# First loads, GpSimd's memsets and the first token copy of a gated scan, in another order

## What is computed

```python
def step(h, xt):
    m = jnp.concatenate([xt, h], axis=-1) @ weight + bias
    c = jnp.tanh(m[:, units:])
    g = jax.nn.sigmoid(m[:, :units] + 1.0)
    return g * h + (1.0 - g) * c, ...
x = x + scan(step, cond, x)
x = x + block(x, cond)
```

## Time and profile before

| | us |
|---|---|
| median of 3 runs | 462.07 |
| lowest and highest of them | 461.28, 463.29 |
| span of the profiled execution | 461.8 |
| busy in it: TensorE | 375.0 |
| VectorE | 304.8 |
| ScalarE | 231.7 |
| GpSimd | 78.5 |

### The profile page before, as it was taken

One profiled execution on the slowest core, in us unless ns is written; L12 is line 12 of the kernel. 1 busy time (PEld: TensorE's weight loads), 2 busy tenths in 40 slices (PEclk: granted clock), 3 DMA queues, 4 the chain that ended last, 5 costly groups with the idle time before them and its releaser, 6 DMA issues.

```text
span 461.8 us, 14117 instructions
## 1 busy us (share of the span) xinstructions
PE 375.0 (81%) x5296; PEld 253.9 (55%) x5296; DVE 304.8 (66%) x1938; ACT 231.7 (50%) x1025; POOL 78.5 (17%) x151
## 2 busy tenths in 40 slices
PE   1999899898857896857898999979599899778832
PEld 1755676566746675746666766636344446446510
DVE  5454444576777776777776676653842378699883
ACT  2123422325335425335446455645688878953952
POOL 7000000012000012000012000032210124266580
PEclk9999999999999999999999999985759989995966
DMA  7200840002000000000000000000000000000102
GB/s 179 62 1 4 181 95 3 2 3 48 1 1 3 1 4 1 2 2 1 2 3 3 1 4 1 2 2 2 3 2 3 1 2 4 1 2 1 23 1 68
DMA packets 9114, 8.42 MB, mean 18 GB/s; under 512 B 1276, under 2 KB 7694, under 8 KB 9047
## 3 DMA queue, kind: packets, MB, share of 16 engines
q1 hardware_dynamic: 8950, 7.26, 7.0%
q0 software_dynamic: 96, 0.26, 0.2%
HBM read 6.45 MB, written 1.08 MB: 16 GB/s over the span
## 4 chain that ended last, share of the span: by engine, by line
PE 56%; DVE 22%; ACT 12%; issue 5%; POOL 2%; DMA 1%; SPq 0%; DVEq 0%; ACTq 0%; POOLq 0%
PE zb L804 21%; PE tb L927 6%; PE zb L782 4%; DVE prod_hi L1569 4%; PE tb L751 4%; ACT state L1265 3%; PE firsts L1098 3%; PE firsts L983 2%; ACT prd L1421 2%; PE tb L898 2%; PE zb L1078 2%; PE firsts L967 2%; ACT state L1268 2%; PE zb L788 2%; PE firsts L804 2%
## 5 line engine op out<-in xcount | busy, mean ns | idle before, releaser
L804 PEld LDWEIGHTS zb<-prod_hi,whh 128*128 128x128 f16 x1920 | 73.7, 106 | 89.9 <-DVE prod_hi L1569 85.8
L1265 ACT ACTIVATE state<-zb 128x8 f32<-128x8 f32 x240 | 42.7, 178 | 152.9 <-PE zb L804 152.4
L804 PE MATMUL zb<-prod_hi,whh 128*128 128x8 f16 x1920 | 91.0, 171 | 34.7 <-DVE prod_hi L1569 34.0
L1569 DVE SCALAR_TENSOR_TENSOR prod_hi<-state 128x16 f16<-128x16 f32 x255 | 44.7, 175 | 83.0 <-ACT state L1268 80.1
L804 PE MATMUL zb<-prod_lo,whh 128*128 128x8 f16 x960 | 63.7, 172 | 0.0
L1575 DVE TENSOR_TENSOR prod_lo<-prod,prod_hi 128x16 f16<-128x16 f32 x255 | 44.7, 175 | 8.7
L1421 ACT ACTIVATE prd<-zb 128x640 f32<-128x640 f32 x64 | 42.2, 712 | 7.8 <-PE zb L1078 7.2
L804 PEld LDWEIGHTS zb<-prod_lo,whh 128*128 128x128 f16 x960 | 44.5, 107 | 0.8
L1571 DVE SCALAR_TENSOR_TENSOR prod<-state 128x16 f32<-128x16 f32 x256 | 43.3, 169 | 0.3 <-ACT state L1268 0.3
L1268 ACT ACTIVATE state<-zb 128x16 f32<-128x16 f32 x240 | 42.8, 178 | 0.0
L1577 DVE SCALAR_TENSOR_TENSOR state<-prod 128x8 f32<-128x8 f32 x256 | 40.8, 159 | 0.0
(11 more groups left out here) (378 smaller groups left out, 708.6 us busy)
## 6 DMA issues: line engine op xcount, KB each, us to landing
mod<-ada_rows SPq DMA_DIRECT2D x4, 768.0 KB, 11.8
resid<-in_x_dram SPq DMA_DIRECT2D x6, 128.0 KB, 3.7
ffz<-shift_rows SPq DMA_DIRECT2D x4, 131.0 KB, 3.3
out_dram<-state SPq DMA_DIRECT2D x8, 64.0 KB, 2.1
out_dram<-early SPq DMA_DIRECT2D x8, 64.0 KB, 2.1
yy<-in_L_cond_w_ada_dram SPq DMA_DIRECT2D x1, 384.0 KB
early<-in_L_cond_weight_dram SPq DMA_DIRECT2D x2, 128.0 KB
resid<-in_x_dram POOLq DMA_DIRECT2D x2, 128.0 KB, 3.5
```

What stands on the lines that cost most here:

```text
L804: i = pe.matmul(z_bank(t, k)[:, NB * (t % CH):NB * (t % CH) + NB], whh[:, half, p, k, :], src[:, NB * p:NB * p + NB], start=False, stop=Fa ...
L1265: act.activation(r[:, 24:32], z_bank(t, 1)[:, k:k + NB], ACT.Tanh, scale=-1.0 / ZS)
L1569: dve.scalar_tensor_tensor(prod_hi[:, :], r[:, 16:32], 1.0, r[:, 0:16], ALU.add, ALU.mult).then_inc(hi_ready, 1)
```

## The change

Five things change, all ahead of step 0.

- The SP queue loads w0x second and cond last of the four; cond counts on its own semaphore, and VectorE waits for the other three alone. TensorE waits for cond, not for the weights.
- The two loads of the tokens of chunk 0 are issued by ScalarE, ahead of its other work, and no longer by GpSimd.
- GpSimd waits for `w_split` after the identities and the small constants. It then clears only the upper nine columns of each head's part of V, without waiting for its own end, and goes on to V's column and O as before.
- `first_x_part` runs the bias matmuls for both gates first, then waits for `xT_first` and runs the token matmuls, gate 1 ahead of gate 0.
- The token copy of chunk 0 is two instructions, one for the first 16 steps (128 columns), which sets `xT_first`, and one for the other 48, which sets `xT_sb`. The wait for `xT_sb` moves into `x_part(0)`.

```diff
@@ sync
             sp.dma_start(w0h[:, :], w0[D:2 * D, :]).then_inc(load_scan, 16)
-            sp.dma_start(condr[:, :], cond).then_inc(load_scan, 16)
+            sp.dma_start(w0x[:, :], w0[0:D, :]).then_inc(load_scan, 16)
             sp.dma_start(b0row[:, :], row(b0)).then_inc(load_scan, 16)
-            sp.dma_start(w0x[:, :], w0[0:D, :]).then_inc(load_scan, 16)
+            sp.dma_start(condr[:, :], cond).then_inc(load_cond, 16)
@@ gpsimd
-            for slot in range(2):
-                tile_dma(pool, x, resid, 0, slot, False).then_inc(load_x0, 16)
...
             pool.memset(half_[:, :], 0.5)
-            settled(pool.memset(V[:, :, :, :, :], 0.0))
+            pool.wait_ge(w_split, 1)
+            pool.memset(V[:, :, :, :, VC:VP], 0.0)
             pool.memset(V[:, :, :, :, HD:HD + 1], C_HEAD)
             pool.memset(O[:, :, :, (NC - 1) * P:NC * P], 0.0).then_inc(pool_init, 1)
@@ tensor, first_x_part
                 for k in range(2):
-                    pe.matmul(z_bank(0, k)[:, 0:n], w0s[:, k, :], xT[:, 0:n], start=True, stop=False,
-                              skip_group_check=True)
                     for half in range(2):
                         pe.matmul(z_bank(0, k)[:, 0:n], b0h[:, half, k, :], onesh[:, 0:n],
-                                  start=False, stop=False, skip_group_check=True)
+                                  start=(half == 0), stop=False, skip_group_check=True)
+                pe.wait_ge(xT_first, 1)
+                for k in (1, 0):
+                    pe.matmul(z_bank(0, k)[:, 0:n], w0s[:, k, :], xT[:, 0:n], start=False, stop=False,
+                              skip_group_check=True)
@@ tensor, x_part
-                        if k == 0 and c and q == 0:
+                        if k == 0 and q == (1 if c == 0 else 0):
                             pe.wait_ge(xT_sb, c + 1)
@@ tensor
-            pe.wait_ge(load_scan, 64)
+            pe.wait_ge(load_cond, 16)
...
             pe.wait_ge(x_split, 1)
-            pe.wait_ge(xT_sb, 1)
             first_x_part()
@@ scalar
+            for slot in range(2):
+                tile_dma(act, x, resid, 0, slot, False).then_inc(load_x0, 16)
...
-            copy_xT(0)
+            act.wait_ge(xT_ps, 1)
+            copy_xT(0, 0, FIRST, xT_first)
+            copy_xT(0, FIRST, CH, xT_sb)
@@ vector
-            dve.wait_ge(load_scan, 64)
+            dve.wait_ge(load_scan, 48)
```

More of the change, by code:

```diff
@@ L364, in ugrnn_block_kernel @@
         NSCAN = sum(1 for g in GROUPS if g[2] < 256)
-        load_scan, load_x0 = sem("load_scan"), sem("load_x0")
+        load_scan, load_x0, load_cond = sem("load_scan"), sem("load_x0"), sem("load_cond")
+        xT_first = sem("xT_first")
         load_x, load_rest = sem("load_x"), sem("load_rest")
@@ L1249, in _, with copy_xT @@
             act.activation(condT[:, :], tb[:, 0, 0:NB], ACT.Copy).then_inc(condT_sb, 1)
-            def copy_xT(c):
-                act.wait_ge(xT_ps, c + 1)
-                first = xT[:, STEPS // NC * NB * c + batch_of(c, 0, 0):][:, 0:1]
+            def copy_xT(c, begin, end, ready):
                 s = batch_of(c, 0, 1) - batch_of(c, 0, 0)
-                act.activation(view(first, [2, NJ], [s, 2], [NB, CH]),
-                               xT_bank(c).rearrange("p (j s t) -> p j s t", j=NJ, s=2),
-                               ACT.Copy).then_inc(xT_sb, 1)
-            copy_xT(0)
+                first = xT[:, NB * (CH * c + begin) + batch_of(c, 0, 0):][:, 0:1]
+                act.activation(view(first, [2, NJ], [s, 2], [NB, end - begin]),
+                               xT_bank(c).rearrange("p (j s t) -> p j s t", j=NJ, s=2)[:, :, :, begin:end],
+                               ACT.Copy).then_inc(ready, 1)
+            act.wait_ge(xT_ps, 1)
+            copy_xT(0, 0, FIRST, xT_first)
+            copy_xT(0, FIRST, CH, xT_sb)
             def step(t):
@@ L1284, in prepare @@
                     yield from at_ticks(now, 26 + 4 * c)
-                    copy_xT(c)
+                    act.wait_ge(xT_ps, c + 1)
+                    copy_xT(c, 0, CH, xT_sb)
                 yield from at_ticks(now, 37)
```

## The result

The changed kernel takes 459.14 us (median of 4 runs, 458.45 to 460.34) against 462.0 (461.28 to 463.29): a ratio of 0.9924, with a 95% interval of 0.9903 to 0.9945. By the ratio that is 3.5 us saved, between 2.5 and 4.5; the two medians lie 2.9 apart. The forecast was 460.1, in a range from 456.3 to 461.2.

The account below looks back on a forecast made before the run. The prediction took a chain of waits ahead of step 0, VectorE shut out by GpSimd memsets, as the bound. Step 0 at 11.25 instead of 13.20 saves 1.95: 461.8 - 1.95 + 0.25 = 460.1 us, range 456.3 to 461.2.

Parts of the forecast that it names:

- T: Moment when the split's loads are in and VectorE starts: 4.1 us chosen, between 3.3 and 5.24.
- rival 2: Cast to prod_hi let in after V's half alone, some 1.5 us earlier than forecast: 458.6 us, chance 0.05.
- The 0.25 that the sum adds: Last term of the sum: the runs' median 462.07 us stands 0.25 above the profiled span of 461.8.
- The split free of memsets: VectorE's scalings and casts before step 0, undisturbed: x_split at T + 1.90, w_split at T + 2.96 us.
- GpSimd's price: GpSimd's memsets behind w_split: 2.25 us for V's half, 1.45 for column and O, ending at T + 6.74.
- The slower rival: V's half costs as much per element as the column: step 0 at 14.4, 463.3 us, chance 0.05.
- The cast is shut out: VectorE's 16-element cast to prod_hi, issued 0.05 us behind GpSimd's memset start, must wait for the memsets.
- Until O is cleared: The cast waits for all three memsets, ending 0.08 us behind O's; step 0 at T + 7.15, or 11.25.
- pool_init, which only attention asks for, tens of us later: GpSimd's signal behind O's clearing: claimed to be needed only tens of us later, by attention.
- rival 1: Cast to prod_hi slips through ahead of the memsets: step 0 at T + 4.05, 457.0 us, chance 0.38.
- Tokens: Chunk 0's token path before step 0: step 0 at 8.7, at worst 9.5, hidden under the wait for the memsets.
- Two-input operations beside a memset: Scan-step operations with two SBUF inputs: cost taken as nothing, since the memsets are over by then.

Follow-up runs that it names:

- after_again: The changed kernel run and profiled again with no edit; ratio 0.9936 against the kernel before.
- memsets_behind_cast: The changed kernel with GpSimd's three memsets waiting for hi_ready instead of w_split; ratio 0.9921 against the kernel before.
- late_and_behind_cast: The changed kernel with GpSimd's memsets waiting for hi_ready and TensorE's wait for pool_init moved to the first scores; 457.73 us, ratio 0.9903.
- memsets_only: The kernel before with only GpSimd's part of the change: wait for w_split, half of V cleared, no settling; ratio 0.9959.
- column_first: The changed kernel with the memsets behind w_split reordered: V's column, O, then V's half; ratio 0.9911 against the kernel before.
- half_in_eight: The changed kernel with V's half cleared in eight memsets, one per batch, instead of one; ratio 0.9956 against the kernel before.

## Why the prediction was right, and where it was wrong

The time fell inside the range, and on the side given 0.60; the single number was 1 us too high. That side was in part luck: 0.55 of the 0.60 stood on a T below 3.75 or on the cast slipping through, and neither happened; the first profile shows rival 2 (let in after V's half), priced at 458.6 and given 0.05. The 0.25 that the sum adds is not the time around the span, which is some 2.1 us; it only makes the sum the median less 1.95. Taken by its steps:

- **The split free of memsets: right.** Eight scalings at 0.21 to 0.23; w_split 2.98 us after the start (forecast 2.96).
- **T: mis-sized.** 4.43, and 4.3 to 4.7 in other runs, where 4.1 was chosen. The transfer's own row, which gave 4.56, was the better guide. The forecast took w0x for the last load; by the chain the last of the three was the bias row, 2.77 us after its issue at 1.64.
- **GpSimd's price: right.** V's half took 2.15 (forecast 2.25), column and O 1.47 from start to end (1.45). The slower rival, a half that costs the column's rate, is out.
- **The cast is shut out: right.** GpSimd started 0.06 behind w_split, the cast was issued 0.07 behind that, and 16 elements were held as 128 were. The row of the 4-element scaling beside the power operation was a poor witness. By the rule of the Trainium skill that the prediction quotes ("SBUF — State Buffer", section "Who interferes with whom") the cast had to wait for the memset in progress, and it did (2.10). The rule speaks of one instruction: by it alone step 0 would stand at T + 5.69, as in rival 2, and not at T + 7.15, as the prediction has it.
- **"Until O is cleared": right in some profiles only.** This step failed for the profile after. Of five profiles with the order half, column, O and no gap, the cast was let in behind the half in three and kept out in two; step 0 of the changed kernel is then at 9.9 or 11.2. The forecast's 11.25 met the second case (11.20 in after_again), but two errors cancel in it: T was 0.22 later than forecast and the way from T to step 0 0.27 shorter. Executions of the first kind would account for the lower median, as would the gains within the scan of the last section, which the forecast did not have; the runs without a profile cannot tell these apart. The step rested on one hand-over, column to O, which kept VectorE out each time it was seen.
- **"pool_init, which only attention asks for, tens of us later": wrong.** It is asked for right behind step 0, so step 1 stood 0.1 behind the end of O. It did not spoil the number, since the forecast had step 0 waiting for O anyway. But it made rival 1 too cheap (rival 2 only by the 0.1 that step 1 lost): with the cast free, step 0 came at 8.17 and the time was that of the changed kernel (memsets_behind_cast). The 457.0 of rival 1 needed the other wait gone as well, and 457.73 is what came then.
- **Tokens: right that they are hidden.** The 2.15 us from x_split to step 0 were too long: with the cast free step 0 started 1.66 us after x_split (8.17 and 8.05, 3.6 us after T), so TensorE was ready by then, where T + 4.05 was forecast. In late_and_behind_cast cond's slack is used up: the transposes behind it end at 6.44, and x_split is in at 6.39.
- **Two-input operations beside a memset: right at nothing**, shown by late_and_behind_cast. The Trainium skill ("SBUF — State Buffer", section "Who interferes with whom") says that such operations collide with GpSimd operations that read SBUF, not with ones that only write it; the traces agree (0.17 and 0.18 beside the memset here, 0.83 beside an operation that reads the earlier trace rows).

## What to carry to other kernels

When work is moved later on an engine, search for every wait on its semaphore and find the place in the waiting engine's own order, not the moment at which the data is used: a wait written at the head of a worker stands behind its first turn. When a long write is moved out of the way of one group of operations, look for operations of the same kind behind the new place. And a gain ahead of a serial chain can be read off the start of an early step, to 0.1 us for one execution, where the whole time scatters by 2 us; but that start can differ between profiles of one program as well (here by 1.2 us), so it takes more than one profile.

## What the runs showed of the hardware that was not expected

- The hand-over between two GpSimd memsets decides whether a waiting VectorE cast gets in. From V's half (2304 elements) to the column it went both ways; from one part of the half (288) to the next, and from O to the half, it got in; from the column (256 single elements) to O it did not, in any of the five profiles in which an operation was waiting. What decides is open; behind V's half it may be the chip (after_again).
- From step 26's first tanh to step 27's lie 1.44 us in the kernel before and 1.13 in the changed one; steps 16 to 48 take 34.98 and 34.99 us in the kernel before and in memsets_only, and 34.56 to 34.70 in all kernels that share the change on ScalarE's side. No wait in the profile accounts for it; it is a part of the gain whose cause was not settled. One thing goes with it: in the kernel before and in memsets_only a packet of the instruction queue q14 is moved 0.6 us behind the late tanh (43.84 to 43.90 in the kernel before), and in the ten profiles that share ScalarE's part it is moved 7 to 8 us ahead of step 26's tanh, where no step is longer. That the one causes the other is not shown.
- The mean step between 50 and 250 is 1.1033 us (1.1032 to 1.1035) in the kernel before and in seven others, and 1.1006 to 1.1011 in four, two of them profiles of the changed kernel, whose remaining profile has 1.1033. That is 0.6 us over the scan, and the three profiles of the changed kernel differ by it. In all four with the shorter step, GpSimd's clearing of O released step 1; in column_first and half_in_eight GpSimd released it too and the step is 1.1034 and 1.1035, so that alone does not decide.
